# Five engines' instruction lists written in another order, in the second half of a two-layer kernel

## What is computed

```python
xn = layernorm(x)                                  # 8192 tokens of 128 features
s = attention(xn)                                  # Q = K = V = xn Wq + bq, in sequences of 512
g = silu(soft_moe(xn))                             # 64 experts of 32 slots
x = x + s * g
xn = layernorm(x)
s = rglru(xn)                                      # h[t] = a[t] h[t-1] + g[t], rmsnorm, W_out
g = silu(channel_mix(xn))                          # mix with the token before, W_r, W_k, W_v
out = x + s * g
```

## Time and profile before

| | before |
|---|---|
| median of 3 runs | 1338.75 us (1338.61 to 1341.29) |
| profiled execution: its time, its span | 1339.13 us, 1337.1 us |
| PE busy, share of the span | 1203.6 us, 90% |
| DVE busy | 1171.3 us, 88% |
| POOL busy | 1015.5 us, 76% |
| ACT busy | 850.1 us, 64% |
| granted TensorE clock, mean | 0.970 |

### The profile page before, as it was taken

How to read it: one execution, slowest core, us unless ns; L and a number is a source line. 1 busy time by engine, 2 the same in 40 slices (tenths; PEclk the granted TensorE clock), 3 DMA queues, 4 the chain that set the end, 5 groups by cost and what they waited for, 6 DMA issues and landing times. The chain is left out here.

```text
span 1337.1 us, 18198 instructions
## 1 busy us (share of the span) xinstructions
PE 1203.6 (90%) x4994; PEld 773.5 (58%) x4994; DVE 1171.3 (88%) x1596; ACT 850.1 (64%) x1675; POOL 1015.5 (76%) x804
## 2 busy tenths in 40 slices
PE   6699999999999999997599898998998998989984
PEld 2365555555555555554276666666666666666651
DVE  6899999999999999997368998888998888998873
ACT  2556565555655555654467777776777777777775
POOL 3499898998988899988478768777768777678630
PEclk9699999999999999999799999999999999999996
DMA  6433333333333333332744333333333333333410
GB/s 199 122 131 134 136 131 142 124 142 125 142 126 140 127 139 138 129 140 107 220 135 134 118 103 127 126 110 127 118 103 126 126 100 129 116 114 112 135 38 16
DMA packets 123221, 167.39 MB, mean 125 GB/s; under 512 B 7153, under 2 KB 99313, under 8 KB 122993
## 3 DMA queue, kind: packets, MB, share of 16 engines
q1 hardware_dynamic: 122688, 164.65, 35.4%
q10 hardware_dynamic: 434, 1.59, 0.3%
HBM read 90.71 MB, written 75.50 MB: 124 GB/s over the span
## 5 line engine op out<-in xcount | busy, mean ns | idle before, releaser
L137 POOL TENSOR_TENSOR exp_slots_loaded<-exp_slots_loaded,slot_max 128x1024 f32<-128x1024 f32 x128 | 319.5, 2517 | 45.7 <-DMA exp_slots_loaded<-exp_slots 45.1
L554 POOL TENSOR_TENSOR dd<-ed,rz 128x512 f32<-128x512 f32 x256 | 263.4, 1050 | 59.5 <-DVE rz L543 59.4
L455 PE MATMUL acc<-dd,xns 128*128 128x512 f32 x512 | 261.0, 592 | 1.3 <-POOL dd L554 1.3
L1205 DVE TENSOR_TENSOR clo<-ct,chi 128x512 fp32r<-128x512 f32 x256 | 172.2, 682 | 38.1 <-ACT chi L1046 37.9
L1046 ACT ACTIVATE chi<-ct 128x512 fp32r<-128x512 f32 x256 | 151.0, 597 | 71.0 <-PE ct L794 70.3
L490 ACT ACTIVATE ed<-lg 128x512 f32<-128x512 f32 x256 | 139.0, 594 | 84.9 <-PE lg L440 84.9
L530 DVE TENSOR_REDUCE mr<-lg 128x32 fp32r<-128x1024 f32 x128 | 154.6, 1208 | 26.1 <-PE lg L426 25.9
L794 PEld LDWEIGHTS ct<-identity,exp_slots_loaded 128*128 128x128 f32 x1024 | 124.5, 142 | 75.3 <-issue 32.6
L562 POOL TENSOR_TENSOR ch<-exp_slots_loaded 128x512 f32<-128x512 f32 x128 | 164.8, 1288 | 0.0
L794 PE MATMUL ct<-identity,exp_slots_loaded 128*128 128x128 f32 x1024 | 149.8, 275 | 15.4 <-DVE clo L1205 12.7
L424 PE MATMUL lg<-phi_transposed,xn_transposed 128*128 128x512 f32 x256 | 157.5, 615 | 2.3 <-PEq L352 1.8
(11 more groups left out here) (190 smaller groups left out, 2500.2 us busy)
## 6 DMA issues: line engine op xcount, KB each, us to landing
exp_slots<-exp_slots_loaded SPq DMA_DIRECT2D x128, 512.0 KB, 2.7
exp_slots_loaded<-exp_slots SPq DMA_DIRECT2D x128, 512.0 KB, 3.5
xns<-xn_rows SPq DMA_DIRECT2D x128, 64.0 KB, 1.7
expert_w<-in_expert_w SPq DMA_DIRECT2D x8, 512.0 KB, 5.0
b_xraw<-in_xT SPq DMA_DIRECT2D x16, 256.0 KB, 3.7
out_t<-b_ti SPq DMA_DIRECT2D x16, 256.0 KB, 2.1
xn_rows<-slot_max SPq DMA_DIRECT2D x2, 1024.0 KB, 5.1
xn_rows<-slot_sum SPq DMA_DIRECT2D x2, 1024.0 KB, 5.3
```

The source lines that it names most:

```text
L137: e.tensor_tensor(rows, rows, joined(SM, b)[:, h].unsqueeze(2).broadcast_to([P, TPB, GC * EPC, NP]), ALU.mult).then_inc(s_we)
L455: e.matmul(acc[k][:, :], xns[w % RX][:, :], dd[w % RX][:, bank(k)], start=tile == 0, stop=tile == NT - 1, skip_group_check=True).then_inc( ...
L554: e.tensor_tensor(dd[v % RX][:, bank(k)].rearrange("q (n p) -> q n p", p=NP), ed[c][:, bank(k)].rearrange("q (n p) -> q n p", p=NP), rz[c] ...
L1205: e.tensor_tensor(clo[c % RC][:, :], ct[c % 2][:, :], hi_f32(chi[c % RC][:, :]), ALU.subtract).then_inc(c_l)
```

## The change

Only the order of the calls in the five loop bodies is changed; every step is still issued once for each block, with the same waits. Some lists also begin at another point of the cycle: where `before` calls a step for block i at the end of a body, the change calls it for i - 1 at the start of the next. A piece of three of the lists:

```diff
                 for i in range(-2, NB + 3):
                     load_x(i - 2)
-                    exps(i - 1, 5)
                     exps(i - 1, 4)
+                    exps(i - 1, 7)
                     exps(i - 1, 6)
-                    exps(i - 1, 7)
                     exps(i, 0)
                     store(i - 3)
                     exps(i, 1)
                     exps(i, 2)
                     exps(i, 3)
+                    exps(i, 5)
...
                     weigh(i, 2)
                     input_gate(i - 1)
+                    combine(i, 11)
+                    decay_gate(i - 1)
+                    turn(i, 3)
+                    ffn_r(i - 1)
+                    exps_turned(i, 14)
                     ffn_k(i - 1)
...
+                    exps_weighed(i - 1, 6)
+                    normalised_low(i - 2)
+                    difference(i - 2)
+                    next_weights(i)
+                    exps_weighed(i - 1, 7)
                     exps_weighed(i, 0)
```

More of the change, by code:

```diff
@@ L1151, in scalar2 @@
                 for i in range(-2, NB + 3):
+                    chunk_high(i - 2, 15)
+                    attended(i - 2)
+                    decay(i - 3)
+                    chunk_high(i - 1, 0)
+                    query(i - 1)
+                    decay_squares(i - 3)
+                    chunk_high(i - 1, 1)
+                    ffn_tanh(i - 3)
+                    chunk_high(i - 1, 2)
+                    y_copy(i - 2)
+                    chunk_high(i - 1, 3)
+                    y_tanh(i - 2)
+                    log_table(i - 1)
+                    input_log(i - 3)
+                    chunk_high(i - 1, 4)
+                    input_root(i - 3)
+                    value_high(i - 1)
+                    chunk_high(i - 1, 5)
+                    probabilities(i - 1, 0)
+                    next_factors(i)
+                    chunk_high(i - 1, 6)
                     state_squares(i - 3)
                     probabilities(i - 1, 1)
+                    chunk_high(i - 1, 7)
+                    probabilities(i - 1, 2)
                     squares(i - 2)
                     state_log(i - 3)
+                    chunk_high(i - 1, 8)
+                    chunk_high(i - 1, 9)
+                    probabilities(i - 1, 3)
                     state_inverse(i - 3)
[L1157 to L1161, removed]
                     deviation_log(i - 2)
                     tanh_table(i - 1)
+                    chunk_high(i - 1, 10)
                     turn_high(i - 1, 0)
-                    chunk_high(i - 1, 10)
                     deviation_inverse(i - 2)
@@ L1171, in scalar2 @@
                     chunk_high(i - 1, 13)
+                    input_tanh(i - 2)
                     decay_tanh(i - 2)
-                    decay(i - 2)
-                    input_tanh(i - 2)
                     turn_high(i - 1, 3)
+                    ffn_r_tanh(i - 2)
                     chunk_high(i - 1, 14)
@@ L1345, in vector2 @@
                 for i in range(-2, NB + 3):
+                    ffn_silu(i - 3)
+                    chunk_low(i - 1, 2)
+                    chunk_low(i - 1, 3)
+                    row_max(i - 1, 0)
+                    silu_y(i - 2)
+                    gated(i - 3)
+                    chunk_low(i - 1, 4)
+                    scan_input(i - 3)
+                    residual(i - 2)
+                    scan(i - 3)
+                    weights(i - 1, 0)
+                    chunk_low(i - 1, 5)
+                    row_max(i - 1, 1)
+                    chunk_low(i - 1, 6)
+                    row_max(i - 1, 2)
                     weights(i - 1, 1)
+                    centre(i - 2)
+                    chunk_low(i - 1, 7)
+                    row_max(i - 1, 3)
                     scaled(i - 1, 0)
-                    row_max(i - 1, 3)
+                    chunk_low(i - 1, 8)
+                    scaled(i - 1, 1)
                     weights(i - 1, 2)
-                    chunk_low(i - 1, 7)
-                    scaled(i - 1, 1)
-                    chunk_low(i - 1, 8)
+                    scaled(i - 1, 2)
                     weights(i - 1, 3)
-                    scaled(i - 1, 2)
                     scaled(i - 1, 3)
+                    state_normalised(i - 3)
                     chunk_low(i - 1, 9)
-                    state_normalised(i - 3)
-                    next_inverse(i)
                     gate_second(i - 3)
@@ L1361, in vector2 @@
                     normalise(i - 2)
+                    output(i - 3)
                     normalised_split(i - 2)
+                    next_inverse(i)
                     chunk_low(i - 1, 11)
-                    output(i - 3)
                     chunk_low(i - 1, 12)
+                    mix_r(i - 2)
                     mix_k(i - 2)
-                    mix_r(i - 2)
                     chunk_low(i - 1, 13)
@@ L1370, in vector2 @@
                     chunk_low(i - 1, 15)
+                    next_max(i + 1)
+                    chunk_low(i, 0)
                     ffn(i - 2)
-                    chunk_low(i, 0)
+                    project_split(i)
                     one_minus(i - 2)
-                    next_max(i + 1)
                     chunk_low(i, 1)
[L1376 to L1392, removed]
             def gpsimd2(e):
@@ L1436, in gpsimd2 @@
                 for i in range(-2, NB + 3):
-                    exps_weighed(i, 0)
[L1438 to L1451, removed]
+                    exps_weighed(i - 1, 1)
+                    exps_weighed(i - 1, 2)
+                    query_low(i - 1)
+                    exps_weighed(i - 1, 3)
+                    gate_attended(i - 2)
+                    next_shifts(i)
+                    exps_weighed(i - 1, 4)
+                    exps_weighed(i - 1, 5)
+                    next_sums(i)
+                    exps_weighed(i - 1, 6)
[3 more added lines that the diff above has]
+                    exps_weighed(i - 1, 7)
+                    exps_weighed(i, 0)
             with nc.Block() as block:
```

64 lines of the change are left out of this document (19 added, 45 removed).

## The result

The changed kernel takes 1291.41 us (median of four runs, 1290.45 to 1292.16) beside 1340.02 for the kernel before on the same chip: ratio 0.9636, 95% interval 0.9619 to 0.9653. The profiled execution's span is 1289.4 us, 47.7 less than that of before.

What follows compares the result with a forecast made beforehand. PE was taken as the bound: 36.7 us busy plus 3.76 waiting a period. New period 38.0, 2.5 less, over fourteen periods 35 us; less 2 for the ends, 33 off 1339.1 gives 1306 us, range 1288 to 1351.

Steps and rivals of the forecast that it cites:

- rival A+: No new wait stays on PE: fourth `scaled` ahead of group 6, `r_ql` in time; period 36.7 to 37, 1291 us; chance 0.16.
- the floor: PE's busy time, 36.7 us a period, taken as the part of the new 38.0 us period that stays.
- the new waits: PE loses 1.0 us a period at the fourth `scaled` and late `chunk_low` 9, and 0.3 for `r_ql`.
- The walk: Step-by-step timing of the new VectorE order against GpSimd's, from the end of cast `r_xh`; new period 38.0 us.
- residual's median 0.7: Sign in the changed kernel's profile: VectorE's residual is not held up, median 0.7 us.
- The scan: VectorE's scan issues 0.2 us ahead of group 4 and takes 1.28 us; gain 1.2 us a period.
- rival B: Scan stays behind group 4 and takes 3.3 us; squares' wait returns with 1.1 a period, 1321 us; chance 0.16.
- the prediction's last sign: The forecast is wrong if PE's busy time itself leaves 36.7 us a period.
- The ends: Last two blocks: later `decay` adds 2 us, bounds 0 and 4; first blocks add nothing, within 3 either way.
- fourteen periods: Fourteen of sixteen `mix_r` and `one_minus` instances are long, so 2.5 us a period counts fourteen times: 35 us.
- C: Residual waits out group 4 and scan group 5, `chunk_low` 5 late for PE; period 41.2 us, 1351 us; chance 0.20.
- D: Waits only change places and PE's waits add up to 3.8 us a period again; 1339 to 1341 us; chance 0.06.

Runs made afterwards that it cites:

- short groups: Kernel before, and changed kernel, each with GpSimd weighing only the first 32 of each 128 x 4 x 256 group: 1268.12 us and 1283.09 us.

## Why the prediction was right

The time, 1291.4, lies in the range (1288 to 1351) and on the side forecast; the likeliest value, 1306, was 15 us too high. The number is that of rival A+ (1291, 0.16), but not its mechanism: A+ wanted no new wait, and PE waits 0.8 us a period, since the fourth `scaled` and the scan still lose in some. That it fits is luck. The period is 36.8 us and not 38.0; of the 1.2 us some 0.7 are the floor and 0.5 the new waits, both below. Over twelve periods that is the whole miss.

**What bounds the kernel: right.** PE's waits were the thing to remove; 45.1 us became 9.2.

**The walk: right to a tenth or two.** VectorE's timeline in one period, after the cast that ends at 1046.37:

```profile
1048.75 1.19 DVE L1271 SCALAR_TENSOR_TENSOR b_xr<-weights,vectors,xn 128x512 f32<-128x512 f32 x1
1049.87 2.87 DVE L1278 SCALAR_TENSOR_TENSOR b_xk<-weights,vectors,xn 128x512 f32<-128x512 f32 x1
...
1058.88 1.12 DVE L1212 CAST r_qh<-b_qf 128x512 fp32r<-128x512 f32 x1
1059.92 0.41 DVE L1289 TENSOR_SCALAR b_a<-b_a 128x512 f32<-128x512 f32 x1
```

and `r_ql` in GpSimd's:

```profile
1060.07 1.40 POOL L1398 TENSOR_TENSOR r_ql<-b_qf,r_qh 128x512 fp32r<-128x512 f32 x1 [0.36 <-DVE r_qh L1212]
```

`mix_r` ended at 3.6 (I said 3.7), `mix_k` at 6.4 (6.4), the cast at 13.6 (13.7), `r_ql` at 15.1 (15.2), and the scan of this period issued at 21.45 (21.4); over the twelve periods the median is 21.5. The last step came right by two misses: `scan_input` was done at 20.4 and not 20.8, and the residual, held up by L111, took 1.22 us and not 0.6, so the sign "residual's median 0.7" failed. `mix_k` kept its wait and PE did not feel it, as forecast.

**The scan: the mechanism right, the margin small.** It was first in nine of twelve periods. Group 4 came at 21.8 at the median (I said 21.6), but anywhere from 21.2 to 23.2, where I had one number. The price of losing, 2.2 us on the period (38.5 against the other nine's 36.2), is above the 1.1 that I gave rival B.

**The new waits: mis-sized.** The fourth `scaled` lost to group 6 in eight of sixteen blocks, where the walk had it in each, and PE waited 1.3 us for it in twelve periods and 3.6 for the late `chunk_low`, 0.4 a period in place of 1.0; and it never waited for `r_ql`, where I had 0.3. The 4.3 us ahead of a T are from the three periods in which the scan lost.

**The floor: mis-sized.** I took PE's busy time, 36.7 us a period, as what PE needs. It fell to 36.0 in the changed kernel and to 35.4 with short groups, where PE waits for nothing. By the prediction's last sign ("if PE's busy time itself leaves 36.7 a period") it is wrong here. Busy time is no fixed amount because one matmul's time in the profile, whose end is modelled, runs into the next one's. PE's timeline in the changed kernel:

```profile
1061.71 0.39 PE L842 MATMUL at<-r_ql,r_qh 128*128 128x512 f32 x1
1061.94 0.39 PE L843 MATMUL at<-r_qh,r_ql 128*128 128x512 f32 x1
```

The second starts 0.23 us after the first, which takes 0.39: 0.16 us lie under both. A wait shorter than that would show as no wait, and a longer one would uncover them and so add 0.16 us of busy time. The 57 waits of the earlier trace rows make some 9 us that way, an estimate, of the 15.8 by which the old order's busy time exceeds that with short groups (440.4 and 424.6). Some 5 more are matmuls that last longer behind a wait (`ffn_k`, L904: mean 645 ns, and 592 with short groups; the same at L910, L922 and L842). The Trainium skill (Trainium Kernel Development and Optimization, Performance Expectations) says that matmul busy time is a bad metric for the distance from the roofline, as matmuls are pipelined; the runs agree, by 1.3 us a period.

**The ends: mis-sized both ways.** Of my fourteen periods one lies ahead of the first `output` and one behind the thirteenth, so the sum had 2.5 us gained ahead and, with the 2 us for the later `decay`, 0.5 gained at the end. The stretch ahead gave 8.9, of which 7.9 come after T0 of block 0, whose scan already takes 1.27 us and not 3.30; the end lost 5.7, and 4.6 of that went with the table loads. Together that is 3.2 where I had 3.0: the two misses cancel, which is luck. The list had been rotated, and I did not check that every index had been.

**The rivals.** B happened in a quarter of the periods. C did not, but one transfer moved made it happen, at 40.7 us a period. D is out: it needed PE's waits to stay.

The rule that who issues first holds the other up (the Trainium skill: SBUF — State Buffer, Who interferes with whom) agrees with each of these: the scan that lost took 3.47 us, which is a group's 2.4 and its own shortest 1.27 less 0.2, and a group that came 0.03 us behind a scan (at 810.25) took 3.42.

## What to carry to other kernels

Where two engines block each other, look for instructions whose median is far above their minimum, and ask which of those an in-order engine behind them feels; the others (`mix_k` here) may stay. A schedule that avoids collisions rests on when transfers land, so move the transfers with it, walk every place where two starts are within a microsecond, and expect a cured collision to turn up at the next instruction. When a software pipeline's list is rotated, go through the index of every call, preloads too: a guard at the ends makes a wrong one cost time without a word.

## What was not expected of the hardware

Two instructions with the same start in the profile, 882.29, and GpSimd's went first. In the traces of the kernel before, of the changed one and of its variants, scan and group 4 start within 0.035 us of each other ten times. In nine the group's start is ahead of the scan's or at most 0.025 us behind it, and the group went first, with a scan of 3.43 to 3.50 us; in the tenth it is 0.033 us behind (810.22 and 810.25 in the changed kernel), and the scan went first.

A load's landing moves with its neighbours: in the changed kernel group 4 became ready anywhere from 0.27 us ahead of the scan's start to 1.69 us behind it, which is what makes three periods long. Load 4 took 4.8 to 6.8 us from issue to landing there, 4.25 at the median when issued 0.9 us later, and 3.39 when held until T5.

A switch between log and exp cost 1.28 us for the load, and the next activation began 0.02 us after it (1244.13 + 1.28 to 1245.43); four loads fewer in the end shortened it by 4.6 us.
